# A Mamba block, experts and a diagonal state space on one core: zero products in TensorE's idle stretches, one expert's weighting sooner, one sum later

## The reference

```python
# 1: selective state space ("attention" in the names)
xs, res = split(x @ Wi + bi); xs = silu(xs)
d_raw, B, C = split(xs @ Wx + bx)
delta = softplus(d_raw @ Wdt + bdt)
h = exp(delta[:, None] * A) * h + (delta * xs)[:, None] * B   # step by step over 512 rows, 256 x 64 states
y = (C * h.sum(states) + xs * Dp) * silu(res)
z = y @ Wo + bo + residual                                    # then a layer norm with gamma, beta
# 2 and 4: experts, the best 2 of 8 weighted
y = sum over e of weight_e * ((silu(x @ W1_e) * (x @ W2_e)) @ W3_e)
# 3: diagonal complex recurrence, 64 states, projected in and out
```

## Time and profile before

| | |
|---|---|
| time, median of 3 runs | 1833.32 us (1830.99 to 1833.5) |
| the profiled execution's own time | 1833.74 us |
| its span, first to last instruction | 1831.9 us |
| mean granted TensorE clock | 0.866 of full speed |
| first scan, last scan ends | 54.4 us, 1664.8 us |
| DMA | 121.89 MB, mean 67 GB/s |

### The profile page before, as it was taken

One profiled execution on the slowest core, in us unless ns is written; L12 is line 12 of the kernel. 1 busy time (PEld: TensorE's weight loads), 2 busy tenths in 40 slices (PEclk: granted clock), 3 DMA queues, 4 the chain that ended last, 5 costly groups with the idle time before them and its releaser, 6 DMA issues. The chain is left out here.

```text
span 1831.9 us, 19041 instructions
## 1 busy us (share of the span) xinstructions
PE 1348.5 (74%) x5928; PEld 612.4 (33%) x5928; DVE 1535.7 (84%) x2154; ACT 1264.5 (69%) x2227; POOL 1497.5 (82%) x876
## 2 busy tenths in 40 slices
PE   5336468678866888778876887768876878668958
PEld 1001123234332433224332343324332343225525
DVE  3999988988899888998999888998999888995232
ACT  4558568777877678786886868777777777664413
POOL 0999989879998799978998899977998899984212
PEclk9556679888998989889897989989898989889969
DMA  3511411131113211122111310132101401100000
GB/s 117 192 52 50 165 46 52 50 123 67 58 47 104 89 52 52 49 92 98 58 46 56 137 52 29 55 109 98 50 32 50 164 29 49 46 29 1 6 1 6
DMA packets 38747, 121.89 MB, mean 67 GB/s; under 512 B 5875, under 2 KB 21110, under 8 KB 26358
## 3 DMA queue, kind: packets, MB, share of 16 engines
q1 hardware_dynamic: 37062, 120.67, 18.5%
q10 hardware_dynamic: 1584, 0.01, 0.0%
HBM read 109.13 MB, written 11.53 MB: 66 GB/s over the span
## 5 line engine op out<-in xcount | busy, mean ns | idle before, releaser
L1275 DVE TENSOR_TENSOR_SCAN h<-da,w 128x512 f32<-128x512 f32 x1024 | 1191.1, 1210 | 111.2 <-ACT da L853 94.5
L956 POOL TENSOR_TENSOR w<-ur,br 128x1024 f32<-128x1024 f32 x512 | 1192.4, 2360 | 29.9 <-DVE h L1275 17.5
L853 ACT ACTIVATE da<-dr,al 128x511 f32<-128x511 f32 x1024 | 680.8, 686 | 245.0 <-DVE h L1275 242.9
L646 PE MATMUL ys<-h,wsum 128*32 128x512 f32 x2048 | 315.4, 692 | 186.7 <-DVE h L1275 167.4
L580 PE MATMUL bankH<-nT,w 128*128 128x512 f32 x512 | 304.5, 679 | 98.5 <-DVE aq L1199 92.8
L899 POOL TENSOR_TENSOR x<-x,yk 128x512 f32<-128x512 f32 x120 | 152.5, 1271 | 181.4 <-ACT yk L815 181.4
L592 PEld LDWEIGHTS bankY<-w,aq 128*128 128x128 f32 x2048 | 250.6, 195 | 85.4 <-issue 75.8
L592 PE MATMUL bankY<-w,aq 128*128 128x128 f32 x2048 | 258.1, 280 | 12.4 <-DVE aq L1199 7.9
L580 PE MATMUL bankG<-nT,w 128*128 128x512 f32 x432 | 249.8, 662 | 16.4 <-DVE aq L1199 16.4
L815 ACT ACTIVATE yk<-bankY,rt 128x128 f32<-128x128 f32 x480 | 140.8, 360 | 86.6 <-PE bankY L592 77.5
L580 PEld LDWEIGHTS bankH<-nT,w 128*128 128x128 f32 x512 | 86.4, 203 | 258.0 <-DVE aq L1199 165.1
(11 more groups left out here) (188 smaller groups left out, 1156.0 us busy)
## 6 DMA issues: line engine op xcount, KB each, us to landing
br<-b_rows SPq DMA_DIRECT2D x64, 1024.0 KB, 5.0
dr<-d_rows SPq DMA_DIRECT2D x16, 1024.0 KB, 7.4
ur<-u_rows SPq DMA_DIRECT2D x16, 1024.0 KB, 8.4
d_rows<-vh SPq DMA_DIRECT2D x16, 256.0 KB
u_rows<-th SPq DMA_DIRECT2D x16, 256.0 KB
xnew<-in_L_attn_a_x_dram SPq DMA_DIRECT2D x8, 256.0 KB, 5.3
w<-in_L_ffn_W_dram SPq DMA_DIRECT2D x2, 1024.0 KB, 11.1
x<-in_L_attn_a_x_dram SPq DMA_DIRECT2D x8, 256.0 KB, 9.0
```

The source lines that it names most:

```text
L646: ins = nc.tensor.matmul(ys[32 * q:32 * q + 32, :], wsum[:, :], h[:, (DUOS * b + 2 * group + q // 2) % H_RING, q % 2, :], start=(n == 0), ...
L853: A(da[duo % D_RING][:, k % 2, 1:L], dr[:, half, q, 1:L], ACT.Exp, scale=nega[:, QUADS * half + q, n:n + 1]).then_inc(decay_ready, 1)
L956: G.tensor_tensor(w[:, turn_duo % W_RING, :, :], ur[:, half, q:q + 2, :], br[:, chunk % B_RING, row:row + 1, :].to_broadcast([128, 2, L]), ...
L1275: V.tensor_tensor_scan(h[:, turn_duo % H_RING, k % 2, :], da[duo % D_RING][:, k % 2, :], w[:, turn_duo % W_RING, k % 2, :], 0.0, ALU.mult, ...
```

## The change

Three edits.

1. At 17 slots of turns 1 to 7, PE issues one more matmul behind that slot's sum, if it has one, and ahead of the slot's other steps. It multiplies a 128 x 32 tile of zeros with `cosT` (128 x 512) and accumulates into partitions 0 to 31 of `ys`, with `start=False`, so the sums stay as they are. It waits for the scan of slot k-3. DVE fills `zeros` once at the start.
2. For expert 3 of the second expert layer `weigh_slot` gives slot 6 for both pairs, where it gave 7 and 8.
3. DVE drains z at slot 8, where it did so at slot 7; its moments follow directly, as before.

```diff
+KEEP_AT, KEEP_LAG = (20, 21, 23, 24, 25, 50, 79, 80, 81, 84, 88, 89, 95, 96, 97, 101, 102), 2
 def weigh_slot(m, e, n):
     at = output_slot(m, e) + WEIGH_LAG
+    if is_late_output(m, e) and e == FIRST_LATE_OUTPUT:
+        return at - 1
     if behind_third(m, e):
...
-        wsum = sb("wsum", [128, 32])
+        wsum = sb("wsum", [128, 32]); zeros = sb("zeros", [128, 32])
...
+                def keep_clock(k):
+
+                    pe.wait_ge(scanned, PAIRS * t.b + k - KEEP_LAG)
+                    nc.tensor.matmul(ys[0:32, :], zeros[:, :], cosT[:, :], start=False, stop=False)
+
                 def pair(k):
-                    if k % 4 != SUM_AT % 4:
-                        return
-                    if k >= SUM_AT:
-                        sum_states(t.b, (k - SUM_AT) // 4)
-                    elif not known(t.b, 1):
-                        sum_states(t.b - 1, PAIRS // 4 - 1)
+                    if k % 4 == SUM_AT % 4:
+                        if k >= SUM_AT:
+                            sum_states(t.b, (k - SUM_AT) // 4)
+                        elif not known(t.b, 1):
+                            sum_states(t.b - 1, PAIRS // 4 - 1)
+                    if k in KEEP_AT and not known(t.b, 1):
+                        keep_clock(k)
...
+            chain(V.memset(zeros[:, :], 0.0))
...
                 yield from take_sums(c, 1, t, TAKE_AT)
-                yield SLOT["z"] + 2
+                yield SLOT["z"] + 3
                 p = got(t, "z")
```

## The result

The changed kernel takes 1821.23 us (median of 5 runs, 1814.72 to 1823.13) against 1830.99 (1830.48 to 1833.5) for the kernel before: a ratio of 0.9931 with a 95% interval of 0.9912 to 0.9949. It is faster by 0.7%, some 10 us by the medians and 13 by the ratio, where 32 had been forecast. The profiled execution of the changed kernel took 1821.23 us, as the median, so the two traces differ by 12.5 us.

A forecast was written before the change was run, and what follows sets the result against it. The time was taken as DVE's work (84% busy) plus waits from its order, POOL close at 82%. Gains 17.4 + 7.8 + 5 + 1.5 = 31.7 us off 1833.74 gave 1802 us, range 1788 to 1824.

The forecast's parts named there:

- how much stays won: Step after z's removed wait: 2.9 us a turn kept over 6 turns, 17.4 us (14.4 to 19.5).
- part 1: Expert 3 weighted sooner and z drained at slot 8, without the zero products: 17.4 us of gain.
- z ends at 633.4: Turn 3: z's matmuls, at full clock, end at 633.4; at the old 5.5 us, 635.0.
- 3.25 us of wait go: DVE's wait ahead of z's drain in turns 2 to 7 vanishes: 3.25 us a turn, or 2.45.
- 3.2 in all: POOL gives back its 2.29 us wait for the moments and 0.93 ahead of nrm, 3.2 us a turn.
- Slots 26 to 52: Warm clock cuts odd turns' waits for decays to the even turns': 70% of 11.2 us, 7.8 us.
- only over slots 28 to 30: Reading of the trace: in the even turn's stretch the clock is down at these slots alone.
- P1, "5 us": First drain of P1 waits less since stepsB runs at full clock, less product 84: 5 us of 10.5 waited.
- Slots 98 to 109: A hole of some 3 us stays and the clock falls in most turns: only 1.5 us gained in all.
- B: Rival: zero products do not hold the clock, part 1 stands; 1823 to 1830 us, likeliest 1823; 15%.
- C: Rival: POOL becomes the bound, DVE waiting for w near slot 26; 1809.5 us; 12%.
- D: Rival: cold products at 84, 95 and 102 delay steps by 1.9 us each; slower, 1856 us; 5%.

The follow-up runs named there:

- part1_only: Kernel before with only the weighting and z's drain moved, no zero products: 1842 us, 11 us slower by the medians.
- part1_padded: part1_only plus three useless DVE scans ahead of z's drain in turns 2 to 7: two groups of runs, 1837.6 to 1843.8 and 1858.9 to 1867.0 us.
- keeps_only: Kernel before with only the zero products added, z at its old place: gains 3.5 us by the medians, 7 by the ratio.
- more_keeps: Changed kernel with zero products at slots 27, 60 and 61 as well, 32 wide: 1807.0 us.
- no_84: Changed kernel without the zero product at slot 84, directly ahead of P1: gains 1.8 us, within the noise.
- best_no84: more2_wide without the product at slot 84: 2.6% faster than the kernel before.
- more2_wide: more_wide with further products, a second at slot 81 and at 93, 99, 100 and 104: 5.3 us slower than best_no84 by the medians.
- keeps_nonzero: Changed kernel with the sums' 0/1 matrix in place of the zeros: 1819.7 us, ratio 0.9934.
- keeps_wide: Changed kernel with zero products 128 wide in place of 32, same slots: 14 us less than the changed kernel.
- more_wide: Changed kernel with products at slots 27, 60 and 61 as well, all 128 wide: 1796.5 us.

## Why the prediction was wrong in its size

The direction, the order of PE's steps and the end of z's wait came as foreseen. The sum did not: 31.7 us forecast, 12.5 between the traces, of which 4.7 in the turns. The step that failed is "how much stays won": part 1's 2.9 us a turn were taken as won with every fall of the clock left at its place, and alone part 1 measures 11 us of loss where 17.4 of gain were forecast.

**Part 1, z.** "z ends at 633.4" (or 635.0) and "3.25 us of wait go": right. PE starts z after 1.37 us of idle, where the prediction allowed 1.3, and the clock is 1.00. Kernel after, turn 3: ACT's two pairs in one row, PE at z, DVE at z and behind it.

```profile
625.02 1.12 ACT L824 ACTIVATE yk<-bankY,rt 128x128 f32<-128x128 f32 x4
```

```profile
626.19 2.05 PE L606 MATMUL bankY<-wo,xd 128*128 128x128 f32 x16 [1.37 <-ACT yk L824]
628.08 1.95 PE L611 MATMUL bankY<-wo,y 128*128 128x128 f32 x16
```

```profile
628.44 2.33 DVE L1285 TENSOR_TENSOR_SCAN h<-da,w 128x512 f32<-128x512 f32 x2
630.69 0.66 DVE L1217 TENSOR_TENSOR z<-bankY,resa 128x512 f32<-128x512 f32 x1
...
639.35 3.20 DVE L1224 TENSOR_SCALAR nrm<-z,rs,nm 128x128 f32<-128x128 f32 x4
```

z's records (two groups of 16) run from 626.19 to 630.03, 3.8 us, as the 3.9 of the prediction said, and DVE finds z ready at 630.69. The turn begins 3.4 us sooner than before, so the end of z, 12.3 us into the turn, is where 633.4 was. ACT's 5.68 us of waiting and POOL's 2.29 went as well, but POOL still waits 0.93 us ahead of its own nrm (the last rows of this text): this share of the "3.2 in all" was not given back.

**"How much stays won? 2.9 us a turn."** Mis-sized first, then lost. Measured from the turn's start, odd turn 3 before and turn 3 after, scan 9 comes 3.37 us sooner, scan 14 2.62, scan 24 2.26, which is 0.6 less than forecast: nrm's longer run takes 1.1 of the first 3.37 (a loss that no step had). From there on the step failed that the prediction never wrote down as one: it kept every fall of the clock where the earlier trace rows show it, and let the products only take falls away. Part 1 moves all that follows by 2 to 3 us, and by that the holes of PE fall otherwise in time: a hole ahead of slot 60 that was harmless at 2.75 and at 2.94 us costs 1.45 us a turn at slot 65 in the kernel after (0.77 to 2.22), and 3.1 in part1_only (to 3.83). In part1_only slot 65 alone waits 27.7 us over turns 1 to 7, where it was 6.6: 21 us, more than the 17.4 that part 1 was to earn. That it is the place of the hole is shown by part1_padded.

**Slots 26 to 52, "I take 70%, 7.8 us".** Measured: slot 32 lost 1.3 us. Its two values of 2.81 and 0.62 became 2.3 in nearly every turn. The products at 20 to 25 are in place and the clock falls anyway at slot 27, through slot 31. The products as such did what they were for: in keeps_only slot 32 waits 0.7 to 0.9 us in five of the turns 1 to 7 (2.3 in turns 4 and 7), 8.5 us in all against 13.4. It is with part 1's shift that the fall lands on slots 27 to 31. One reading was wrong as well: in even turns the clock is down over slots 20 to 25 too and not "only over slots 28 to 30" (turn 4 of the kernel before):

```profile
870.60:877.20 6.60, 5.62 (x24) 3.69 (x24) 6.29 (x7) 4.94 (x12) 6.44 (x6) 0.50 0.01 2
```

So an even turn was not a turn whose thin stretch had been held warm, but one in which a fall came earlier, at slots where it cost less. The prediction saw that x1T's and lg1's thin stretch "may still fall badly" and put it at 30% of odd turns; it was 6 turns of 7. Slots 54 and 56 did gain, 4 us, since 50 to 52 stay at full clock. The Trainium skill, "TensorE: Matmul & The Clock Gate", Part 4, says that a transpose doesn't count as busy for the clock in the way a matmul does; that a fall behind the transposes stays, from slot 27 or 28 on in keeps_only too, agrees with it. But its rule is not the only one that fits, since with product 27 the fall is gone in more_keeps and slot 32 waits 0.13 us, and no run here set a transpose against a matmul.

**P1, "5 us".** Measured: 2.0 (10.5 to 8.5). stepsB runs at full clock (two products in 1.98 us and not 3.78, at 752.20 in turn 3), as forecast. The wait left is 1.03 us in most turns, which is product 84 itself, and without it (no_84) it is 0 in turns 1 to 6 (1.86 in the last), yet the kernel gains only 1.8 us, within the noise: its turns 2 to 6 stay at 208.1 to 208.3, because P1's 1.03 us come back at slot 109 (0.96 to 2.2 us), where the falls moved to 103 to 107. In best_no84, with more holes behind filled, they stay won: 0.72 us in each of six turns by P1's wait, 4.3 in all, and 5.3 us against more2_wide by the medians (but their ratios' intervals overlap).

**Slots 98 to 109, "1.5 us".** Measured 5.9, more than the 4.5 of its best case: here the forecast was too careful, and the clock falls for two stretches of some 3 us rather than through ten slots.

**The rivals.** *B*, that zero products don't hold the clock, is refuted: with the products on top of part 1 the clock is 0.901 and not 0.858, stepsB runs at full clock and the time is 21 us less (part1_only against the kernel after). It took two properties together. Zeros: of no weight, by keeps_nonzero. "They fill 32 of 128 output columns": real in part, 14 us by keeps_wide and 10 by more_wide against more_keeps, with the middle width between. The prediction weighed B by the first property and by what the Trainium skill, "TensorE: Matmul & The Clock Gate", Part 1, says of zeros and the peak-current limiter, and so never priced the second. Its row for it, that the clock comes back behind sums that are also 32 wide, was of four products side by side, not of one. *C*, POOL: the wait ahead of slot 26 is 1.20 us as before in all the kernels with either part, and POOL follows a turn of 202.3 us in best_no84, so it doesn't bind. *D*, cold products ahead of three steps: of its three only 84 holds anything up in most turns, and by 1.03 us, not 1.9 (in turn 6 of the kernel after, where the clock is down, P1 waits 2.5 and the x drain at slot 96 0.7).

What stays open: why a given hole brings the clock down at one time and not at another, beyond that its place counts; how much of the 12.5 us is chance ahead of the first scan and behind the last; how much of the width's gain comes through the 0.1 us that each product shifts, since no run kept the timing and changed the width alone; and the second group of part1_padded.

## What to carry to other kernels

Where an engine's clock falls behind thin stretches of its own work, a microsecond taken out of a chain moves all later work against the clock, and may bring it down at places that were fine: price such a change with the falls free to move, and fill every thin stretch of the turn before taking waits away, or the parts will be judged one by one as useless. Make filling products as wide as the array (here it paid, though part of it may be a shift in time), and look for the step that stands directly behind each one. When a wait that was removed doesn't show in the time, list the same engine's waits by slot before and after; the sums over the run hide a loss of one place in the gain of another.

## What the runs showed of the hardware

*The clock falls at short holes, by their place.* 2.75 and 2.94 us of idle PE in the kernel before left it at 1.00, 2.95 in the kernel after and in part1_only brought 0.50, and with 2.94 in part1_padded it was 1.00 again. The turns settle at nearly equal lengths, whatever work is added or taken away: 208.33, 208.09, 208.11 and 208.17 us in turns 2 to 5 of the kernel after, 208.14 to 208.27 in turns 2 to 6 with product 84 gone, and 211.63 to 211.67 in part1_padded with 4.84 us more of DVE work in each. Why at these lengths, no run shows.

*The width of a filling product counts, its data doesn't.* 1807.0, 1801.5 and 1796.5 us, at a mean clock of 0.917, 0.921 and 0.923, with 32, 64 and 128 columns, whether by the clock itself or by the 0.1 us that each product shifts; 1819.7 with the sums' weights, a matrix with ones in it, in place of zeros, and 1821.2 with zeros.

*A tensor_scalar on DVE ended only when POOL's instruction had ended.* The four nrm instructions took 2.09 us in the kernel before and 3.20 after, all of it in the first. POOL in the kernel after, turn 3:

```profile
639.33 2.37 POOL L965 TENSOR_TENSOR w<-ur,br 128x1024 f32<-128x1024 f32 x1
642.63 1.27 POOL L917 TENSOR_TENSOR nrm<-nrm,bcs 128x512 f32<-128x512 f32 x1 [0.93 <-DVE nrm L1224]
```

w runs to 641.70, and the first nrm, started at 639.35, ends at 641.78 after 2.43 us; the other three take 0.33 each. Before, nrm started 1.1 us into a w, at 646.07, and ended 0.08 us behind it. It is so in all of turns 1 to 7: the first nrm takes 1.32 us before and 2.36 to 2.43 after. So it costs what is left of POOL's instruction, and part 1 moved nrm to the beginning of one. The Trainium skill, "SBUF — State Buffer", section "SBUF: two separate sides", says that a DVE operation in a two-port mode and a GpSimd operation lock one pair of ports against each other for a whole instruction; these numbers agree, though no trace shows in which mode nrm ran. It was only read from the traces; no run moved nrm by itself.
